# The fp8 adjacency of a graph-attention layer: loaded by converting transfers from GpSimd's queue instead of cast on ScalarE

## What is computed

```python
h = jnp.maximum(_layernorm(x, axis=-1), 0.0)
x = x + _L0_gnn_ref(h, adj, W, a, wtrans)       # graph attention
# inside L0: e = leaky_relu(Wh1 + Wh2.T); mask = adj > 0
# attention = softmax(where(mask, e, -1e12)); negative = -softmax(where(mask, -e, -1e12))
# elu(concat([attention @ h, negative @ h]) @ wtrans)
...                                             # L1: D^-1/2 adj D^-1/2 h W + b, relu
...                                             # L2: adj @ (sign features @ sign weights), relu
...                                             # L3: (1-t) h W + t adj @ (h W)
```

## Time and profile before

| | |
|---|---|
| device time, median of 3 runs | 1042.36 us (1040.41 to 1042.6) |
| the profiled execution, its own time | 1043.36 us |
| its span | 1041.7 us |
| PE busy | 981.4 us (94%) |
| DVE busy | 761.0 us (73%) |
| ACT busy | 529.6 us (51%) |
| POOL busy | 45.7 us (4%) |
| HBM read and written | 128.72 MB, 14.50 MB |

### The profile page before, as it was taken

One profiled execution on the slowest core, in us unless ns is written; L12 is line 12 of the kernel. 1 busy time (PEld: TensorE's weight loads), 2 busy tenths in 40 slices (PEclk: granted clock), 3 DMA queues, 4 the chain that ended last, 5 costly groups with the idle time before them and its releaser, 6 DMA issues.

```text
span 1041.7 us, 20921 instructions
## 1 busy us (share of the span) xinstructions
PE 981.4 (94%) x7549; PEld 708.9 (68%) x7549; DVE 761.0 (73%) x1143; ACT 529.6 (51%) x879; POOL 45.7 (4%) x96
## 2 busy tenths in 40 slices
PE   5779899999999999999999699999999999999996
PEld 4437588888888888888887145555568874555553
DVE  5467889889898988988898665556566775555553
ACT  4477888887888888898877622222220001111110
POOL 2000000000000000000003000000003330000000
PEclk7688899999999999999999779999999999999998
DMA  6002343434433443343444124555554446666661
GB/s 229 1 12 83 93 135 113 136 123 124 127 95 117 125 131 114 98 139 110 126 120 139 46 97 169 194 196 171 189 191 171 146 149 195 204 207 213 216 216 60
DMA packets 36556, 143.73 MB, mean 138 GB/s; under 512 B 4236, under 2 KB 17701, under 8 KB 36389
## 3 DMA queue, kind: packets, MB, share of 16 engines
q1 hardware_dynamic: 35285, 142.37, 41.9%
q10 hardware_dynamic: 1232, 0.85, 0.3%
HBM read 128.72 MB, written 14.50 MB: 137 GB/s over the span
## 4 chain that ended last, share of the span: by engine, by line
PE 46%; ACT 21%; DVE 20%; issue 10%; DMA 1%; DVEq 1%; ACTq 0%; POOL 0%; POOLq 0%
PE f_ya L1245 34%; ACT f_gb L938 12%; DVE f_s_mat L1430 6%; DVE f_s_mat L1435 5%; ACT f_s_mat L948 5%; PE f_yb L1162 5%; DVE f_wm L1426 3%; DVE f_gb L1427 3%; PE f_ya L1133 2%; ACT f_a L960 2%; PE f_yb L1156 1%; PE f_ya L1172 1%; PE f_yb L1172 1%; DMA f_ident<-ident_dram 1%; PE f_yb L1133 1%
## 5 line engine op out<-in xcount | busy, mean ns | idle before, releaser
L1172 PE MATMUL f_ya<-f_x_mat,f_s_mat 128*128 128x257 f16 x2028 | 351.9, 272 | 8.5 <-DVE f_s_mat L1435 7.8
L1172 PE MATMUL f_yb<-f_x_mat,f_s_mat 128*128 128x257 f16 x2028 | 334.2, 273 | 0.0
L1245 PE MATMUL f_ya<-f_x_mat,f_a 128*128 128x512 f16 x1352 | 324.3, 385 | 9.5 <-DVE f_x_mat L1493 9.4
L1245 PEld LDWEIGHTS f_ya<-f_x_mat,f_a 128*128 128x128 fp8e4 x1352 | 132.4, 99 | 149.7 <-DVE f_x_mat L1493 16.4
L1172 PEld LDWEIGHTS f_yb<-f_x_mat,f_s_mat 128*128 128x128 f16 x2028 | 196.3, 97 | 28.9
L1172 PEld LDWEIGHTS f_ya<-f_x_mat,f_s_mat 128*128 128x128 f16 x2028 | 149.8, 97 | 29.0 <-issue 10.4
L938 ACT ACTIVATE f_gb<-f_e_tile,f_expc 128x256 f32<-128x256 f32 x338 | 140.3, 497 | 24.6 <-DVE f_s_mat L1435 23.8
L1430 DVE SCALAR_TENSOR_TENSOR f_s_mat<-f_wm,f_s_mat 128x1792 f16<-128x1792 f32 (+1 forms) x52 | 98.4, 1892 | 32.3 <-ACT f_s_mat L948 30.9
L1175 PE MATMUL f_ya<-f_ones,f_a 128*128 128x1 f16 x676 | 111.9, 166 | 0.0
L1569 DVE SCALAR_TENSOR_TENSOR f_gb<-f_gb 128x1664 f32<-128x1664 f32 x52 | 98.0, 1887 | 11.9 <-DVE f_s_mat L1619 11.9
L1426 DVE TENSOR_TENSOR f_wm<-f_gb,f_a 128x1792 f32<-128x1792 f32 (+1 forms) x52 | 98.1, 1887 | 1.8 <-issue 0.8
(11 more groups left out here) (138 smaller groups left out, 740.4 us busy)
## 6 DMA issues: line engine op xcount, KB each, us to landing
f_gb<-adj_dram SPq DMA_DIRECT2D x52, 832.0 KB, 5.3
f_a<-f_a_dram SPq DMA_DIRECT2D x39, 832.0 KB, 4.4
f_a<-adj_t_dram SPq DMA_DIRECT2D x26, 896.0 KB, 5.0
f_a<-adj_t_dram SPq DMA_DIRECT2D x26, 768.0 KB, 4.6
f_a_dram<-f_a SPq DMA_DIRECT2D x26, 224.0 KB, 5.2
f_a_dram<-f_a SPq DMA_DIRECT2D x26, 192.0 KB, 4.6
out_dram<-f_s_mat SPq DMA_DIRECT2D x25, 128.0 KB, 4.5
f_xs<-x_dram SPq DMA_DIRECT2D x3, 768.0 KB, 9.1
```

The lines of the kernel that those rows point to most:

```text
L1172: return pe.matmul(bank[:, 0:F + 1], s_mat[:, j, side, i], x_mat[:, j, x_side, 0:F + 1], start=start, stop=stop)
L1245: return pe.matmul(bank_a[p][:, 0:W], a8_pair[:, r, at:at + P], x_layer[layer][:, j, 0:W], start=(j == 0), stop=(j == TILES - 1))
```

## The change

The f32 adjacency is loaded a second time, straight into `a8`, by 52 transfers on GpSimd's queue that convert f32 to fp8 as they move the data. ScalarE's cast and its semaphore go; `a8_here[c]` takes the place of `cast_done` for the PE and for SP's stores. GpSimd waits for `et_done` before the first four, then for `s_free` of the chunk that used this part of `a8` and for the store of it. These waits stand in GpSimd's order ahead of the three inverse roots of layer 1. SP's `load_chunk` waits for `wp_done` alone. ScalarE's order in a pair becomes: the highs of this chunk, (at c = 1) the ELU exponentials, then the products of the next chunk; in pair 0 only the casts are taken out.

```diff
@@ SP
 def store_a8(m, c):
     lo, hi = CHUNKS[c]
+    wait(a8_here[c], 16 * (m + 1))
     sp.dma_start(a8_dram[...], a8[:, lo:hi, :]...).then_inc(a8_stored[c], 16)
...
     if not (start and c < 2):
-        wait(cast_done, n - 1)
         wait(wp_done, n - 1)
     load_chunk(m, c)
...
     for c in (2, 3):
-        wait(cast_done, NC * (PAIRS - 1) + c + 1)
         store_a8(PAIRS - 1, c)
@@ GpSimd, between the inverse roots of LN0 and of LN1
+def load_a8(m, c):
+    lo, hi = CHUNKS[c]
+    if not isinstance(m, int) or m > 0:
+        g.wait_ge(s_free, NC * m + c - NC + 1)
+        g.sem_inc(waited, 1)
+        g.wait_ge(a8_stored[c], 16 * m)
+        g.sem_inc(waited, 1)
+    g.dma_start(a8[:, lo:hi, :], adj_t[m, :, lo:hi, :])\
+     .then_inc(a8_here[c], 16)
+
+g.wait_ge(et_done, 2)
+for m in range(PAIRS):
+    for c in range(NC):
+        load_a8(m, c)
@@ ScalarE
-def cast(m, k, c):
-    ...
-    a.activation(a8[:, lo:hi, :], blocks(a32, c), ACT.Copy, saturate=False).then_inc(cast_done, 1)
...
     for c in range(NC):
-        if c < NC - 1:
-            products(m, r, k, c + 1)
         if c == NC - 1:
             divide(m - 1, 1 - r)
-            if not known or m < PAIRS - 1:
-                products(m + 1, 1 - r, k + r, 0)
         highs(m, c)
-        cast(m, k, c)
         if c == 1 and (not known or m > 1):
             for p in range(2):
                 elu_exp(2 * m - 4 + p, p)
+        if c < NC - 1:
+            products(m, r, k, c + 1)
+        elif not known or m < PAIRS - 1:
+            products(m + 1, 1 - r, k + r, 0)
@@ PE, both places
-pe.wait_ge(cast_done, n + 1)
+pe.wait_ge(a8_here[c], 16 * m + 16)
```

More of the change, by code:

```diff
@@ L627, in fast_program @@
         hp_done = sem("hp_done")
-        cast_done = sem("cast_done")
+        a8_here = [sem(f"a8_here{c}") for c in range(NC)]
         check_here = [sem(f"check_here{i}") for i in range(2)]
@@ L988, in first_pair @@
                         highs(0, c)
-                        cast(0, 0, c)
                     products(0, 0, 0, 2)
@@ L993, in first_pair @@
                     highs(0, 2)
-                    cast(0, 0, 2)
                     products(1, 1, 0, 0)
                     highs(0, 3)
-                    cast(0, 0, 3)
                     x0_high(3)
```

## The result

| | before | after |
|---|---|---|
| device time, median | 1041.89 us (1040.41 to 1042.6, 4 runs) | 1030.72 us (1028.39 to 1032.03, 4 runs) |
| the profiled execution, its own time | 1043.36 us | 1028.39 us |
| its span | 1041.7 us | 1026.8 us |

The kernel is 11.2 us faster, a ratio of 0.9898 [0.988, 0.9915]; the median of before has one run more than the 1042.36 above. The two profiled executions are 15.0 us apart, since that of before lies above its median and that of after is the fastest of its four.

A forecast was written before the change was run, and what follows sets the result against it. The DVE's order, with its waits for ACT, was taken as the bound at 36.94 us a pair. Attention's -15.6 and the start's +1.6 gave -14.0, from 1042.4 to 1028.4 us, with a range of 1024.5 to 1050.

The forecast's parts named there:

- The period: Attention's four chunks on the DVE: 8.90, 7.98, 8.73 and 9.95 us, so 35.56 instead of 36.94, 1.38 less.
- From period to end: Attention to the last blocks: 15.6 us saved over the pairs, divisors of pair 12 at 569.7, the 12.4 us behind unchanged.
- start loss: At `et_done`, four loads start beside the reload of the exponentials, which lands late: 1.6 us lost, bounds 0 and 4.8.
- Casts gone, highs first: ACT's attention work without casts and with highs ahead of products: 1.38 us saved a full period, 15.6 us in all.
- GpSimd's order: Layer 1's inverse roots behind all 52 loads: root ends at 541.2, wanted at 546.2, so 5.0 us of cover.
- The conversions: The 52 converting loads into `a8`: landing between 5.0 and 12.2 us, lower end taken, hidden under 26 us of cover.
- 217 GB/s: DMA rate in attention with the second load: 7.8 MB a pair in 35.9 us, near what layer 3 runs at.
- Rival B: At PE's wait for `a8_here`, converting transfers don't keep up and the kernel is slower, 1062 us; chance 0.20.
- Rival C: GpSimd's issue of loads holds up the DVE: about 1073 us, or 1033 at 0.1 a load; dear case chance 0.04.
- port rule: DVE and GpSimd share a port pair, so descriptor making would hold, or be held by, the DVE; a trace row shows little.
- Rival D: In attention, the new wait for products eats the old wait for highs; only start loss left, 1042 to 1044; chance 0.09.
- Rival E: GpSimd reaches layer 1's roots over 5 us later than forecast, each us counting: 1029 to 1036 us; chance 0.07.

The follow-up runs named there:

- e2: The kernel before with ScalarE's new order and the cast last, behind the products, no second load: 1027.22 us, ratio 0.986.
- e12: The kernel after again, unchanged, as a base for its group, four conversions starting beside the tiles of exponentials: 1030.48 us, ratio 0.9893.
- e10: The kernel after with GpSimd waiting for both tiles of exponentials before its first load, run again as a base: 1025.6 us, ratio 0.9842.
- e4: The kernel after once more, unchanged, on the chip of the first group: 1030.81 us, ratio 0.989.
- e3: The kernel after, with GpSimd waiting until both tiles of exponentials have landed before its first load: 1025.76 us, ratio 0.9856.
- gated kernel: The kernel after, with GpSimd waiting until both tiles of exponentials have landed before its first load: 1025.76, 1026.6 and 1025.6 us in three groups.
- e5: The kernel after with GpSimd's first load behind both tiles of exponentials, run again as the base of its group: 1026.6 us, ratio 0.9849.
- e7: The gated kernel with layer 1's first inverse root taken twice on GpSimd: 1029.41 us, ratio 0.988.
- e6: The gated kernel with every part of `a8` loaded twice, the second time when the first has landed: 1039.17 us, ratio 0.9978.
- e8: The kernel before with the highs first, then the cast, ahead of the ELU exponentials and the next products: 1084.48 us, ratio 1.0401.
- e1: The kernel after with ScalarE's old order, products of the next chunk ahead of the highs, and no cast: 1039.77 us, ratio 0.9988.
- e11: The kernel before with the new order and the cast last, no second load, run again: 1026.54 us, ratio 0.9851.
- e9: The kernel after with GpSimd's wait for both tiles of exponentials behind its first conversion, so one starts beside them: 1025.3 us, ratio 0.9835.

## Why the prediction was right, and the term that was mis-sized

*The period.* Forecast 35.56, measured 35.59. By chunks: 8.90, 7.98, 8.73, 9.95 against 8.89, 8.06, 8.72, 9.92. The new wait for products in chunk 3 was to be 1.1 us and is 1.11; the signal from ACT to the DVE, for which I had estimated 0.14, took 0.25 there (products end at 295.93, L1428 starts at 296.18), and the chunk is 0.08 over. The lows were to be free of waits and kept nine of 0.16 us, one a pair.

*From period to end.* From the last `weigh` matmuls of the PE, which follow its gap of 5 us (113.94 in the timeline of before, 114.23 in that of after), to its last blocks it was 483.71 us and is 468.05, 15.66 less; forecast 15.6. The divisors of pair 12 were to come at 569.7 with a start loss still to be added, and came at 569.90; the 12.4 us behind them stayed. The PE ended attention at 567.05 (forecast 567.8), so it is not yet the bound. e2, with the order alone, has the same period, so the mechanism is the forecast's: its *Casts gone, highs first* takes both together, and it is the second that counts.

*The start loss* is the term that was mis-sized: 1.6 us (bounds 0 and 4.8) where the medians show 4.9 (e12 less e10) and 5.05 (e4 less e3), just past the upper bound. I had made it of two parts, and neither came so. The store was to be stretched and to delay the loads by 2.3 us; they were issued at 54.70, 2.1 us after the store (52.59), as in before (52.70 and 54.76). The landing was to take 6.7 us, by the factor of 2.1 of one crowded row; the first tile took 8.3 (8.9 in e4, 8.5 in e12). The two errors nearly cancel, 63.8 forecast and ACT's start at 63.06 measured, so that the idle time of 0.89 to 1.76 us is near the 1.6 partly by luck. What the term left out is that the loss does not end with this idle time: of the 4.1 us between the mean spans only 2.0 are there at the first attention matmul. Without this loss the gated kernel is 15.0, 15.5 and 16.4 us under its before (e3, e5, e10), around the 15.6 of the sum. My number of 1028.4 is 2.3 us low; the 3.3 us that this term lacks cover that, and the others came out together within 1 us.

*The tile and the queues.* First the rows: the tile is issued by SP and the conversions by GpSimd, on queues of their own, and still the tiles took three times as long. The Trainium skill (DMA: Bandwidth & Descriptors, "Issuing engines are not separate DMA queues") says that transfers of all issuing engines share the same 16 DMA engines; the trace agrees, and it was this rule that spoke for a start loss above 0.

*GpSimd's order.* The cover of the root was to be 5.0 us; it is 5.2 (546.45 less 541.26), and e7 confirms it by using it up. The root itself took 8.69 us here and not 9.24.

*The conversions.* They land in 5.8 and 4.6 us (I took 5.0, with 12.2 as the far end), and PE never waits for them. By queue q0's 13.3% of 16 engines over 1026.8 us, 137 us for 44.3 MB of source, they move 324 GB/s counted by what they read. The 217 GB/s that I wanted to see does not stand in a window as such, since the packets' count takes the written side of a conversion. The window from 250 to 490 us of after has (packets and bytes of all queues, then of q0):

```profile
DMA packets 12604, 35.74 MB, mean 149 GB/s; under 512 B 1392, under 2 KB 9072, under 8 KB 12604
...
q0 software_dynamic: 3744, 5.54, 28.4%
```

With four bytes read for each one that q0 wrote, 16.6 MB more, this is 218 GB/s. The other transfers became slower, the f32 loads 6.1 and 5.1 us instead of 5.0 and 4.6, under their cover.

*Rival B* (conversions don't keep up) is down for this kernel, but e6 shows the margin: it bears one conversion a chunk and not two in sequence, and what breaks first is GpSimd's order with its roots, not the PE's wait at which I had put the price.

*Rival C* (issue holds the DVE) is down: an issue takes 0.53 us on GpSimd, and the DVE's instructions take 2.02 and 1.76 us as before. The page of the profile has the mean of L1426 of before and L1428 of after at 1887 and 1888 ns. The port rule that I had cited for this rival made no difference that these times show.

*Rival D* (nothing to gain) was right in what it described, a wait for one thing in place of another, and wrong in size: 1.11 us took the place of 1.5 in chunk 3, and of nothing elsewhere; in e8's order the new wait does eat everything, and more. *Rival E* did not come in this kernel, and came in e6 and e7.

## What to carry to other kernels

When one engine waits for another that is not saturated, look at what stands ahead of the wanted instruction in the other's order before moving work off it. Here the new order alone gave the whole gain (e2). The removed cast alone, in the old order, gave 4 us behind the start, of which the median kept 1 (e1), and the same cast one place earlier cost 42 us (e8). The second load of 44.3 MB on top of the right order is worth 0.9 to 1.5 us at best (e10 and e3 against e11 and e2), within what the intervals leave open, and it makes the kernel 4 us slower than without it (e4 and e12 against e2 and e11) if four bulk transfers start just as a small load on the critical path is due. If it is kept, it should wait for that small load: e9, e10, e3 and e5, at 1025.3 to 1026.6 us, beat both kernels of the case.

## What the runs showed that I had not expected

- Two loads of 128 KB, issued together, land in 3.2 to 3.9 us (median of the two) with no bulk transfer beside them, in 4.8 beside one transfer of 896 KB of source, and in 9.2 to 10.0 beside four, although these are on another engine's queue.
- A conversion of f32 to fp8 takes about as long as a plain load of the f32 that it reads: 5.8 us for 896 KB, beside 6.1 for the plain load of the same 896 KB in the same kernel.
- An idle time of 0.9 to 1.8 us early in the kernel went with 4.9 and 5.05 us in the medians. Where the part behind the first attention matmul comes from stays open.
- With its loads and roots in one order, GpSimd's roots set the end (e6, e7) while the transfers themselves still kept up.
